# One core, gated cross-attention with switched heads: both weightings and the sums over heads in one section of TensorE's order

## The reference

```python
x = x + jnp.tanh(g_xattn[0]) * xattn(ctx, ctx, layernorm(x), mask, wq, bq, wk, bk, wv, bv, wo, bo)
...
q, k = einsum('btc,hdc->bhtd', x, Wq), einsum('btc,hdc->bhtd', x, Wk)      # 16 heads of 64
mix_v = the sigmoids of each head's 2 best gates x @ Ws, else 0            # b t h e
v = einsum('bthe,bted->bhtd', mix_v, einsum('btc,edc->bted', x, Wv))
attn = einsum('bhij,bhjd->bihd', softmax(q @ k / 8), v)
mask_o = 1 for each head's 2 best gates x @ Wd, else 0                     # b t h e
res = einsum('bthe,bthd,efd->bthf', mask_o, attn, Wo).sum(axis=2)          # sum over heads
x = x + jnp.tanh(g_ffn[0]) * res
```

## Time and profile before

| | us |
|---|---|
| runs, median of 3 (lowest to highest) | 1252.23 (1251.17 to 1255.26) |
| profiled execution | 1245.54 |
| its span, first to last instruction | 1243.8 |
| TensorE busy | 1188.9 |
| DVE, ScalarE, POOL busy | 902.1, 620.0, 550.7 |

### The profile page before, as it was taken

The page is one execution under the profiler, slowest core; times in us unless marked ns, Lnnn a source line. Parts: engine busy times, 40 slices in busy tenths (PEclk is TensorE's granted clock), DMA queues, the critical chain, the costliest instruction groups (busy, mean ns, idle before and its releaser), DMA issues. The chain is left out here.

```text
span 1243.8 us, 41871 instructions
## 1 busy us (share of the span) xinstructions
PE 1188.9 (96%) x16568; PEld 947.7 (76%) x16568; DVE 902.1 (73%) x2556; ACT 620.0 (50%) x1481; POOL 550.7 (44%) x821
## 2 busy tenths in 40 slices
PE   5699999999999999999879999999999999999995
PEld 4477777777777777777557888888888888888874
DVE  3477777777877777777757877777877777787763
ACT  3366666666666666665434444434444444443431
POOL 3476777677777767777611122122122212212120
PEclk9899999999999999999999999999999999999998
DMA  8899998888778878877315656656666665665663
GB/s 229 193 203 199 207 201 201 178 187 185 179 179 186 183 177 186 178 175 159 69 50 127 163 140 145 152 140 149 148 157 142 137 167 145 142 155 139 148 149 94
DMA packets 263010, 200.31 MB, mean 161 GB/s; under 512 B 195934, under 2 KB 243872, under 8 KB 258720
## 3 DMA queue, kind: packets, MB, share of 16 engines
q1 hardware_dynamic: 262816, 197.64, 70.2%
HBM read 125.49 MB, written 72.11 MB: 159 GB/s over the span
## 5 line engine op out<-in xcount | busy, mean ns | idle before, releaser
L899 POOL TENSOR_SCALAR shifted<-raw,neg_max 112x375 f32<-112x375 f32 x512 | 327.3, 649 | 163.5 <-DVE neg_max L781 120.3
L781 DVE CUSTOM_DVE_ANT_0 raw<-bank_s,maskb 112x375 f32<-112x375 f32 x512 | 266.6, 544 | 103.0 <-issue 87.8
L686 ACT ACTIVATE probsT<-bank_t 128x512 f32<-128x512 f32 (+3 forms) x512 | 189.1, 458 | 104.1 <-PE bank_t L460 104.1
L447 PE MATMUL bank_s<-K_stack,Q_stack 128*112 128x375 bf16 x512 | 150.8, 335 | 5.0 <-DVE neg_max L781 4.7
L1444 DVE TENSOR_REDUCE max<-bank_s 112x4 f32<-112x448 f32 x128 | 78.8, 615 | 71.6 <-PE bank_s L1201 71.6
L460 PEld LDWEIGHTS bank_t<-ident,shifted 48*128 48x128 f32 (+1 forms) x3072 | 105.3, 139 | 27.8 <-issue 24.2
L460 PE MATMUL bank_t<-ident,shifted 48*128 48x48 f32 (+1 forms) x3072 | 122.6, 226 | 0.0
L1537 POOL TENSOR_TENSOR mix_bd<-pm_te,tok 128x448 f32<-128x448 f32 x32 | 31.5, 986 | 200.5 <-DMA pm_te<-pm_dram 200.5
L1153 PE MATMUL bank_ab<-xnT,wq2T 128*128 128x224 f32 x512 | 109.4, 357 | 0.7 <-ACT qT L1337 0.6
L1153 PE MATMUL bank_ab<-xnT,wk2T 128*128 128x224 f32 x512 | 109.6, 357 | 0.0
L203 POOL TENSOR_SCALAR var_eps<-moments 112x1 f32<-112x1 f32 x32 | 7.2, 224 | 227.0 <-DVE moments L199 226.8
(11 more groups left out here) (147 smaller groups left out, 2191.8 us busy)
## 6 DMA issues: line engine op xcount, KB each, us to landing
K_stack<-k_dram SPq DMA_DIRECT2D x64, 562.5 KB, 7.8
k_dram<-k_parts SPq DMA_DIRECT2D x32, 562.5 KB, 4.4
att_dram<-att_q SPq DMA_DIRECT2D x31, 511.0 KB, 3.9
att_th<-att_dram SPq DMA_DIRECT2D x31, 511.0 KB, 4.3
v_dram<-mv SPq DMA_DIRECT2D x32, 455.0 KB, 6.5
v<-v_dram SPq DMA_DIRECT2D x32, 455.0 KB, 4.0
K_stack<-k_dram SPq DMA_DIRECT2D x32, 375.0 KB, 9.2
Q_stack<-q_dram SPq DMA_DIRECT2D x64, 168.0 KB, 9.1
```

The source lines that it names most:

```text
L447: nc.tensor.matmul(bank_s[h % 2][0:S, 0:S2], Q_stack[:, p, h, :], K_stack[:, p, h, :], start=True, stop=True).then_inc(scores_ready, 1)
L686: act.activation(probsT[:, g % 2, first_u:end, lo:hi], bank_t[0:KP, bank, column:column + (end - first_u) * (hi - lo)].rearrange("p (u q) ...
L781: dve.tensor_tensor_reduce(raw[:, g % 2, j, :], bank_s[h % 2][0:S, 0:S2], c.maskb[:, :], -1.0, -LEAST, ALU.add, ALU.min, neg_max[:, g % 2, ...
L899: pool.tensor_scalar(shifted[:, g % 2, j, 0:S2], raw[:, g % 2, j, :], -1.0, neg_max[:, g % 2, j:j + 1], ALU.mult, ALU.add).then_inc(shift_ ...
```

## The change

The two weighings of a batch stand next to each other in TensorE's order, ahead of sum_heads. Both wait for the exponentials of both halves. In the second half, the eighth head's 65 columns are split: 57 (FITS) fill up the bank in bank_g, and 8 go to bank_t, in a step of their own, `weigh_rest`. It comes behind sum_heads(b - 1), or ahead of it in the last iteration. sum_heads waits for the first of the copies of (b, 0), weigh_rest for both. pv_done of the second half is signalled by weigh_rest. A batch has five attention copies instead of four, and ScalarE makes all of them behind copy_fill(b, 2).

```diff
+        ATT_COPIES = (2, 3)
+        ATT_BATCH = sum(ATT_COPIES)
+        TAIL_AT, FITS = 2 * G * (S - D), PSUM_BANK - (2 * G - 1) * W
         def weighed(half, m):
-            return bank_g[:, half, m * W:(m + 1) * W] if m < 7 else bank_t[:, 1, 2 * G * (S - D):2 * G * (S - D) + W]
+            if m + 1 < 2 * G:
+                return [(bank_g[:, half, m * W:(m + 1) * W], 0, W)]
+            if half == 0:
+                return [(bank_t[:, 1, TAIL_AT:TAIL_AT + W], 0, W)]
+            return [(bank_g[:, 1, m * W:PSUM_BANK], 0, FITS), (bank_t[:, 1, TAIL_AT + W:TAIL_AT + 2 * W - FITS], FITS, W)]
...
             def turn(b, half):
                 pe.wait_ge(shift_done, NG * b + 2 * half + 2)
                 wait(pe, exp_done, 2 * (2 * b + half))
-                wait(pe, att_copied, 2 * (2 * b + half))
+                wait(pe, att_copied, ATT_BATCH * b)
...
                 pe.wait_ge(mv_copied, 2 * min(b + 2, B))
-                wait(pe, att_copied, 2 * (2 * b + half))
-                pe.wait_ge(exp_done, 2 * (2 * b + half) + 2)
+                wait(pe, att_copied, ATT_BATCH * b)
+                pe.wait_ge(exp_done, 2 * (2 * b + 1) + 2)
                 for m in range(2 * G):
-                    for lo, hi in HALVES:
-                        last = nc.tensor.matmul(weighed(half, m)[lo:hi, :], probsT[:, half, m, lo:hi], v[:, p, 2 * G * half + m, :], start=True, stop=True)
-                last.then_inc(pv_done, 1)
+                    last = weigh_head(b, half, m, weighed(half, m)[0])
+                if half == 0:
+                    last.then_inc(pv_done, 1)
+
+            def weigh_head(b, half, m, place):
+                dst, first, end = place
+                for lo, hi in HALVES:
+                    last = nc.tensor.matmul(dst[lo:hi, :], probsT[:, half, m, lo:hi], v[:, b % 2, 2 * G * half + m, first:end], start=True, stop=True)
+                return last
+
+            def weigh_rest(b):
+                pe.wait_ge(att_copied, ATT_BATCH * b + ATT_COPIES[0])
+                weigh_head(b, 1, 2 * G - 1, weighed(1, 2 * G - 1)[1]).then_inc(pv_done, 1)
...
-                pe.wait_ge(att_copied, min(4 * b + 6, 4 * B))
+                pe.wait_ge(att_copied, min(ATT_BATCH * (b + 1) + 1, ATT_BATCH * B))
...
                 fill(b, 0)
-                weigh(b, 0)
...
                 fill(b, 2)
+                weigh(b, 0)
                 weigh(b, 1)
+                if b + 1 == B:
+                    weigh_rest(b)
                 if b > 0:
                     sum_heads(b - 1)
+                if b + 1 < B:
+                    weigh_rest(b)
...
-                act.activation(att_q[:, b % 4, first + 7, 0:W], weighed(half, 7)[0:S, :], ACT.Copy).then_inc(att_copied, 1)
+                for src, at, end in weighed(half, 2 * G - 1):
+                    act.activation(att_q[:, b % 4, first + 7, at:end], src[0:S, :], ACT.Copy).then_inc(att_copied, 1)
...
                 copy_fill(b, 0)
-                copy_attention(b, 0)
...
                 copy_fill(b, 2)
+                copy_attention(b, 0)
                 copy_attention(b, 1)
```

More of the change, by code:

```diff
@@ L1077, in store_attention @@
                 sp.wait_ge(pick_done, b + 1)
-                sp.wait_ge(att_copied, 4 * b + 4)
+                sp.wait_ge(att_copied, ATT_BATCH * (b + 1))
                 sp.dma_start(att_dram[b], att_q[:, b % 4, :, :].rearrange("s h w -> s (h w)")).then_inc(att_stored[p], 16)
@@ L1182, in mix_values @@
                 wait(pe, u_copied, b - 2)
-                wait(pe, att_copied, 4 * (b - 1))
+                wait(pe, att_copied, ATT_BATCH * (b - 1))
                 wait(pe, mv_copied, 2 * b)
```

## The result

| | before | changed |
|---|---|---|
| runs, median (lowest to highest) | 1252.05 us (1246.53 to 1255.85), 8 runs | 1260.91 us (1258.65 to 1267.97), 8 runs |
| profiled execution | 1245.54 | 1259.39 |

The ratio is 1.0082, 95% interval 1.0052 to 1.0112. In microseconds that is +8.9, where +4.9 was forecast. Between the two profiled executions it is +13.9. The ratio compares the medians of the runs; the two profiled executions are single ones, and how far those scatter turned out to be a finding of its own.

What follows compares the result with a forecast made beforehand. TensorE, busy 96% of the span, bounds some thirty iterations, waits the tail. -4.9 + 3.1 + 3.8 + 2.9 = +4.9 us on the profiled 1245.5 gives 1250.4; the runs' median offset of 6.7 makes 1257.1, range 1250 to 1264.

Steps and rivals of the forecast that it cites:

- the loop through DRAM: Values and pm stored and loaded through SP's queue until mix_bd; a later attention exchange lengthens it, +3.8 us of stalls.
- TensorE's own pace: Steady iterations: one section of split tiles less, -4.9 us, against four added instructions for the split head, +3.1 us.
- Make_proj's 0.17: make_proj behind a fill instead of a weighing: 1.73 us instead of 1.90, in 29 iterations, -4.9 us.
- The opening of a weighing: Weight loads idle 0.28 us before each weighing; taken as costing 0, at the other end a gain of 8.1 us.
- rival 2: A weighing's opening has a hidden price; at 0.34 us the saved section gives 9.9 more, 1247.2 us; chance 0.10.
- the 8 columns: Split head's four added instructions per iteration, taken at 0.12 us; bounds 0.07 and 0.55; +3.1 us over 28 iterations.
- The loop's stalls: Mixing waits for mix_bd in about half the iterations: 4.5 us in place of 0.7, +3.8, bounds 0 to +8.0.
- The slack of 0.8 us: Mean time from mix_bd's end to the next mixing over 28 iterations of the profile; under 0.4 in twelve.
- Rival 4: Loop through DRAM has less slack in timed runs than profiled: +8 us for the term, 1261 us; chance 0.15.
- The later exchange: Attention copies end nearer the next iteration, store and load 0.9 us later; values' load at 9.2 to 10.
- New waits: sum_heads waits for the first copy of (b, 0), weigh_rest for the second; both covered by weighings or sums, 0.
- The tail: Iterations 30 and 31: weighings move onto the path, +1.1 and +1.5, rest and third copy +0.3; +2.9, bounds 2.4 to 3.6.

Runs made afterwards that it cites:

- the first trace: Changed kernel as first profiled, its execution taking 1259.39 us; the kernel before's first profiled execution took 1245.54.
- the pairs of one chip: Unaltered kernels before and changed, profiled again side by side: second traces 1257.07 and 1264.95 us, third traces, on one more chip, 1265.52 and 1277.55.
- the first two traces: First profiled executions of the kernel before and the changed kernel: 1245.54 and 1259.39 us.
- the three pairs: Before and changed kernel, unaltered, profiled three times each: 1245.54 and 1259.39, 1257.07 and 1264.95, 1265.52 and 1277.55 us.
- the kernels with the loop off the path: Before, changed and combined orders with SP storing pm ahead of the values' load; before 1244.41, changed 1243.18, combined 1239.97 us, or 1245.47 with the change's tail.
- the second trace before: Kernel before, unaltered, profiled again: 1257.07 us; 18 runs on that chip had a median of 1253.24.
- the first two traces before: Kernel before, unaltered, profiled twice: 1245.54 and 1257.07 us.

## Why the prediction was right, and where its sum was off

The forecast was slower by more than 0.3%, at 1257.1 within 1250 to 1264, and the measured 1260.9 lies in that range. The step that I had weighed most, the loop through DRAM, is what decided it: the kernel that only takes it away is faster by 0.5 to 0.6% in either order. But the terms of the sum were off in both directions, and that their errors offset each other is luck: TensorE's own gain was 5 us larger than forecast, the stalls grew by 5 to 13 us more.

- **TensorE's own pace**, forecast -4.9 + 3.1 = -1.8 us, was -0.25 x 28 = -7.0. Make_proj's 0.17 was right. The opening of a weighing, which I took at 0 and kept as rival 2 (0.28 to 0.34), costs 0.15: the chain had it inside the weighing's piece. Against sum_heads' 33 ns per instruction, 0.96 + 0.12 for 31 was already 35, which is 0.05 us, a third of it, and I didn't add that up. By the drain rule of the Trainium skill (TensorEngine Tiling (Array Packing), Key Properties) both changes of mode cost; the trace now agrees with it, at 0.15 on the way in and 0.18 on the way back. And the 8 columns cost 0.06 to 0.07, not 0.12. The Trainium skill's floor (TensorE: Matmul & The Clock Gate, "Wait — 56ns, not 53.3ns?") of about 25 ns per instruction gives an estimate of 0.10; the measured 16 ns each in two column halves is below it, and the measurement decides.
- **The loop's stalls**, forecast 4.5 in place of 0.7, are 17.6, 16.5 and 26.1 in place of 0.8, 7.3 and 13.3. They grew by 16.8, 9.2 and 12.8 us where I had +3.8. The mechanism was right, the size was not, for two reasons. The slack of 0.8 us was that of one quick execution. And each iteration of TensorE's work was 0.19 us shorter than I had it: where the loop sets the pace, that turns into waiting, up to 5 us over 28 iterations. My rival 2 overlooked this too, as it counted such a gain in full, down to 1247.2. Rival 4 (less slack in the timed runs) had said so, with 1261; it was the best number in the text, at a chance of 0.15. The profiled execution's 6.7 us below the median was the hint; I drew on it only there, and in the sum carried it over as a constant. And the fit was looser than I wrote: 0.16 us is the standard deviation of the 28 pairs from the line, not their limit, the furthest is 0.38 away, and for the end of mix_bd it is 0.46 and up to 0.97.
- **The later exchange.** The values' load was forecast at 9.2 to 10 after the mixing's start, and is at 9.2 in the mean of the first trace, with the attention's load at +0.3. The 0.9 us that I took for how much later it comes was too much: 0.50 between the first traces, and 0.04 and 0.20 in the pairs of one chip, as in those traces SP's queue holds the exchange back in the kernel before as well. There the loop grew by only 0.13 to 0.20 us per iteration. Since the loop sets the period, the sums of both terms belong together: forecast -1.8 + 3.8 = +2.0, measured +3.7 and +4.8, and +12.3 between the first two traces, of which the one before had a quick loop.
- **New waits** were forecast at nothing, and in the steady iterations of the changed kernel's traces there are none: no idle time of the sums ends with a copy.
- **The tail**, forecast +2.9 (2.4 to 3.6): +1.9, +2.7 and +4.7 in the three pairs, over +6 in the kernels with the loop off the path. The two weighings on the path are as described. The +1.1 for iteration 30 didn't show in the first pair, where it ran at 1.00 against 0.88; iteration 31 gave +2.3 up to the last exchange, for a forecast of +1.8. I had nothing for a lower clock in the tail, which the later traces have.

What stays open. The kernel with the exchange early and no wait for the 8 columns took 1260.44 us; its trace has iterations 2 to 29 at 518.6 us, 1.7 less than the second trace before, and a tail 1.9 us longer, which leaves nothing of its +7. Against the mean of the first two traces before, which lie on both sides of the median, it is +2.1 in the iterations, +3.3 in the tail and +2.6 ahead of the second mixing. The second mixing, up to which these kernels hardly differ, starts between 654.1 and 659.8 us from run to run, and I can't say whether the later values of the changed ones are chance. That the late exchange by itself was worth +8.3 us in the order of before, while only 4.1 us stand in its trace against the second trace before, is open as well, for the same reason: single traces scatter by more. How a transfer beside the values' store slows it was seen only as a correlation (0.9 us for 1 us, in 28 iterations); it wasn't tested by itself. Nor do the runs share out the loss between the later exchange and TensorE's shorter iteration.

## What to carry to other kernels

A gain on the busiest engine is worth nothing where a loop through DRAM closes in the same time: before counting it, compare each such loop's length with the iteration as it will be after the gain, not as it is. And read that slack from more than one execution, above all if the profiled one is quicker than the median; here two more traces of the same kernel left 0.2 us of the 0.8. Looking into the queue that the loop runs through paid more than the reordering: one store that waited behind another's landing without need was worth 0.5%, in a few moved lines.

## What the runs showed of the hardware that I had not expected

- A section of matmuls on half of the columns has a price at its start as well as at its end: 0.15 us in and 0.18 us back to the whole array, at a granted clock of 1.00.
- fp32 matmuls with 8 columns moving, with loads of 64 and 48 columns, cost about 16 ns each where column halves alternate.
- Three executions of one kernel, on at least two chips, took 1245.5, 1257.1 and 1265.5 us, with its loop of DMAs at 17.5, 18.3 and 18.6; the four kernels with the loop off the path that were timed had medians of 1240.0 to 1245.5, three on one chip and one on the other.
